# The first stage's pointwise product in three one-pass products of high and low parts, the image's low part made by VectorE

## The reference

```
xp = star_scale * square(relu(xn @ w_pw1.T)) + star_bias     # 128 -> 256 channels, the pointwise product
xf = rfft2(xp)                                               # goes on to a filter, an inverse, w_pw2
r  = relu(conv1x1(relu(conv1x1(xn, rw_fc1)), rw_conv))       # routing branch, its mean is used
s  = relu(conv3x3(xn, sp_fc1))                               # routing branch, its mean is used
```

## Time and profile before

| | before |
|---|---|
| runs | 391.28, 391.15, 389.53 us; median 391.15 |
| profiled execution, its own time | 390.03 us |
| its span on the core | 388.0 us |
| mean granted TensorE clock | 0.945 |
| TensorE busy | 84% of the span |
| VectorE / ScalarE / GpSimd busy | 59% / 44% / 57% |

### The profile page before, as it was taken

The page is one execution under the profiler, slowest core; times in us unless marked ns, Lnnn a source line. Parts: engine busy times, 40 slices in busy tenths (PEclk is TensorE's granted clock), DMA queues, the critical chain, the costliest instruction groups (busy, mean ns, idle before and its releaser), DMA issues.

```text
span 388.0 us, 7237 instructions
## 1 busy us (share of the span) xinstructions
PE 327.7 (84%) x2135; PEld 273.7 (71%) x2135; DVE 228.3 (59%) x700; ACT 170.7 (44%) x346; POOL 219.9 (57%) x257
## 2 busy tenths in 40 slices
PE   1899999995289999889685599979999999999930
PEld 0566665622158888768574599979999999999920
DVE  2376555346264479897967148785555455546844
ACT  1355544422212443328342244435645444546833
POOL 3375344030386863888877770077777777644550
PEclk9999999999589999989989699989999999999985
DMA  7990000003622324705221421123433222228535
GB/s 213 308 237 15 3 0 0 0 3 88 134 54 57 83 60 175 254 29 190 58 76 56 112 77 42 29 76 87 122 90 90 83 84 82 77 62 273 184 107 189
DMA packets 26073, 38.37 MB, mean 99 GB/s; under 512 B 5508, under 2 KB 16280, under 8 KB 25512
## 3 DMA queue, kind: packets, MB, share of 16 engines
q1 hardware_dynamic: 20408, 28.64, 26.2%
q0 software_dynamic: 4320, 8.92, 6.9%
q10 hardware_dynamic: 1312, 0.40, 0.7%
HBM read 22.16 MB, written 12.60 MB: 90 GB/s over the span
## 4 chain that ended last, share of the span: by engine, by line
PE 70%; DVE 9%; POOL 7%; DMA 6%; issue 4%; SPq 1%; ACT 1%; ACTq 0%; POOLq 0%; DVEq 0%
PE psum L1110 18%; PE psum L1094 11%; PE psum L899 8%; POOL xs_dram L641 6%; PE psum L1087 5%; PE psum L992 4%; PE psum L880 4%; PE psum L888 3%; PE psum L965 3%; PE psum L1004 2%; DMA rwc<-in_rwc 2%; PE psum L1079 2%; PE psum L911 1%; PE psum L936 1%; PE psum L986 1%
## 5 line engine op out<-in xcount | busy, mean ns | idle before, releaser
L670 POOL DMA_INDIRECT y_dram<-spec,idx_scatter x71 | 69.4, 978 | 35.1 <-issue 17.4
L641 POOL DMA_INDIRECT xs_dram<-images,idx_dispatch x64 | 62.5, 976 | 36.9 <-DVE idx_dispatch L1382 18.5
L1110 PE MATMUL psum<-RS,xgt_hl 128*128 x142 | 52.7, 371 | 6.6 <-DVE shared L1500 5.6
L817 ACT ACTIVATE shared<-psum 128x384 f32<-128x384 f32 x71 | 34.4, 489 | 46.1 <-PE psum L1110 45.9
L1500 DVE TENSOR_TENSOR shared<-shared,psum 128x384 f32<-128x384 f32 x71 | 38.3, 552 | 26.0 <-ACT shared L817 25.8
L1110 PE MATMUL psum<-w_hi,xgt_hl 128*128 x142 | 49.4, 348 | 0.0
L1506 DVE COPY spec<-psum 128x256 f32<-128x256 f32 (+1 forms) x36 | 15.1, 420 | 41.4 <-PE psum L1079 28.3
L1110 PE MATMUL psum<-w_lo,xgt_hl 128*128 x142 | 38.2, 351 | 0.0
L568 POOL TENSOR_TENSOR buf<-star 128x512 f32<-128x512 f32 (+1 forms) x8 | 10.1, 1267 | 44.9 <-DVE star L1174 44.9
L1110 PEld LDWEIGHTS psum<-RS,xgt_hl 128*128 128x128 f32 x142 | 28.1, 198 | 8.1 <-issue 8.1
L965 PE MATMUL psum<-RS,coef 128*128 128x512 f32 x48 | 20.9, 511 | 14.6 <-DMA RS<-r_dram 11.4
(11 more groups left out here) (195 smaller groups left out, 647.8 us busy)
## 6 DMA issues: line engine op xcount, KB each, us to landing
shared<-xs_dram SPq DMA_DIRECT2D x71, 65.0 KB, 1.8
star<-in_w SPq DMA_DIRECT2D x2, 1536.0 KB, 8.9
rw<-spec SPq DMA_DIRECT2D x8, 256.0 KB, 3.8
turned_b<-spec SPq DMA_DIRECT2D x8, 256.0 KB, 4.2
images<-y_dram SPq DMA_DIRECT2D x8, 256.0 KB, 4.3
out<-T SPq DMA_DIRECT2D x8, 256.0 KB, 2.0
spec<-in_w SPq DMA_DIRECT2D x1, 1536.0 KB, 6.5
shared<-in_sp_even SPq DMA_DIRECT2D x1, 1280.0 KB, 14.2
```

Of the source, the lines that this page charges most:

```text
L641: pool.indirect_dma_start(xs_dram, bass.IndirectOffsetOnAxis(ap=idx_dispatch[:, b, k, t:t + 1], axis=0), XR[:, 2 * b + t // 4, t % 4, :], ...
L670: pool.indirect_dma_start(y_dram, bass.IndirectOffsetOnAxis(ap=idx_scatter[:, j:j + 1], axis=0), yo[:, b * P:b * P + P], None).then_inc(S[ ...
L817: act.activation(silu[j % 2], p_h1[j % 2][:, 0:HID], ACT.Silu).then_inc(S["f_silu"], 1)
L1110: mm = pe.matmul(h[:, 0:HID], xgt[j // 2 % 2][xs][:, j % 2 * P:j % 2 * P + P], w_hl[ws][:, cols], start=(n == 0), stop=(n == 2))
```

## The change

`wp1` is split once into `wp1_hi` (ScalarE, a copy that rounds to `fp32r`) and `wp1_lo` (VectorE, the difference). Each pair's image is split the same way: ScalarE's first copy (L698) now writes `xc_hi` as `fp32r`, and a new VectorE operation `image_low` subtracts it from the interior of the padded image `xp` and writes the low part into `r_hl`, whose own use comes later. `image_low(i+1)` stands on VectorE between `stats(i+2)` and `spectrum_copy(i)`. `star_matmul` waits for the low part (`a_xl`) where it waited for `a_xc`, and has three products where it had one. The first routing product reads `xp`'s interior where it read `xc`. `wp1`'s transfer gets a semaphore of its own (`wp_in`); ScalarE waits for it before `image(0, 0)`, VectorE does `wp1_lo` and `image_low(0, 0)` between stats and normalise of pair 1, and TensorE waits for `wp_lo` once.

```diff
+        wp1_lo = sb("wp1_lo", [P, MED], F32R)          # in wp1's place
+        xp_s = sb("xp_s", [P, 4 * PAD * PAD + PAIRS * PIX])
+        xc_hi = sb("xc_hi", [P, 1024], F32R)
+        wp1_hl = [sb("wp1_hi", [P, MED], F32R), wp1_lo]
+        xc_hl = [xc_hi[:, :].rearrange("p (u n) -> p u n", u=2), r_hl[:].rearrange("p u f m -> p u (f m)")]
...
-        CONSTS = 16 * 8
+        CONSTS = 16 * 7
+        TERMS = ((0, 0), (0, 1), (1, 0))
...
             def image(i, u):
-                act.activation(xc[:, u, :], ps_tr[:, :], ACT.Copy).then_inc(S["a_xc"], 1)
+                act.activation(xc_hl[0][:, u, :], ps_tr[:, :], ACT.Copy).then_inc(S["a_xc"], 1)
...
             act.wait_ge(S["pad_zero"], 1)
+            act.wait_ge(S["wp_in"], 16)
+            act.activation(wp1_hl[0][:, :], wp1[:, :], ACT.Copy).then_inc(S["wp_hi"], 1)
             image(0, 0)
...
             def star_matmul(i, u):
-                pe.wait_ge(S["a_xc"], i + 1)
+                pe.wait_ge(S["a_xl"], i + 1)
                 for j in range(2):
                     wait_done(pe, S["a_relu"], i * 2 + j - 1)
                     for g in range(2):
-                        mm = pe.matmul(ps_pw[j][:, g * MED:(g + 1) * MED],
-                                       xc[:, u, (2 * g + j) * P:(2 * g + j + 1) * P], wp1[:, :], start=True, stop=True)
+                        for n, (xs, ws) in enumerate(TERMS):
+                            mm = pe.matmul(ps_pw[j][:, g * MED:(g + 1) * MED],
+                                           xc_hl[xs][:, u, (2 * g + j) * P:(2 * g + j + 1) * P], wp1_hl[ws][:, :],
+                                           start=(n == 0), stop=(n == 2))
                     mm.then_inc(S["a_pw"], 1)
...
-                                   xc[:, u, g * PIX:(g + 1) * PIX], start=True, stop=True)
+                                   xp[:, u, g, 1:SIZE + 1, 1:SIZE + 1], start=True, stop=True)
...
             pe.wait_ge(S["consts_in"], CONSTS)
+            pe.wait_ge(S["wp_lo"], 1)
             pair_loop(pe, phase_a)
...
+            def image_low(i, u):
+                dve.wait_ge(S["a_xp"], i + 1)
+                dve.wait_ge(S["a_xc"], i + 1)
+                wait_done(dve, S["a_rw1"], i - 1)
+                rows_of = "p (g a b) -> p g a b"
+                dve.tensor_tensor(xc_hl[1][:, u, :].rearrange(rows_of, g=2, a=SIZE), xp[:, u, :, 1:SIZE + 1, 1:SIZE + 1],
+                                  xc_hl[0][:, u, :].rearrange(rows_of, g=2, a=SIZE).bitcast(F32), ALU.subtract)\
+                    .then_inc(S["a_xl"], 1)
...
                     stats("a", i + 2, u)
+                if not last(i, PAIRS):
+                    image_low(i + 1, 1 - u)
+                if not deferred(i):
                     spectrum_copy(i)
...
             stats("a", 1, 1)
+            dve.wait_ge(S["wp_hi"], 1)
+            dve.tensor_tensor(wp1_hl[1][:, :], wp1[:, :], wp1_hl[0][:, :].bitcast(F32), ALU.subtract).then_inc(S["wp_lo"], 1)
+            image_low(0, 0)
             normalise("a", 1, 1)
```

More of the change, by code:

```diff
@@ L198, in metaformer @@
         route_b = sb("route_b", [P, NF * P])
-        wp1 = sb("wp1", [P, MED])
+        with nc.sbuf_tensor("wp1", [P, MED], F32) as wp1:
+            pass
+        wp1_lo = sb("wp1_lo", [P, MED], F32R)
         wp2 = sb("wp2", [P, 2, DIM])
@@ L228, in metaformer @@
         xn = sb("xn", [P, 2, 4, DIM])
-        images = sb("images", [P, 4 * PAD * PAD + PAIRS * PIX + 1024])
+        with nc.sbuf_tensor("images", [P, 4 * PAD * PAD + PAIRS * PIX + 1024], F32) as images:
+            pass
+        xp_s = sb("xp_s", [P, 4 * PAD * PAD + PAIRS * PIX])
+        xc_hi = sb("xc_hi", [P, 1024], F32R)
+        wp1_hl = [sb("wp1_hi", [P, MED], F32R), wp1_lo]
         s_from, xc_from = 4 * PAD * PAD, 4 * PAD * PAD + PAIRS * PIX
-        xp = images[:, 0:s_from].rearrange("p (u g a b) -> p u g a b", u=2, g=2, a=PAD)
-        s_all = images[:, s_from:xc_from].rearrange("p (i a b) -> p i a b", i=PAIRS, a=SIZE)
-        xc = images[:, xc_from:].rearrange("p (u n) -> p u n", u=2)
+        xp = xp_s[:, 0:s_from].rearrange("p (u g a b) -> p u g a b", u=2, g=2, a=PAD)
+        s_all = xp_s[:, s_from:xc_from].rearrange("p (i a b) -> p i a b", i=PAIRS, a=SIZE)
         XR = images[:, 0:TILES * ROW].rearrange("p (i q r) -> p i q r", q=4, r=ROW)
@@ L350, in metaformer @@
             "ident_in consts_in tab_in x_in0 x_in1 x_in2 x_in3 route_in w1_in w3_in w2_in w_hi w_lo pad_zero coef_zero mhalf_set coef_ps "
-            "coef_hi coef_lo coef_in a_stats a_aggr a_eps a_rstd a_norm a_tr a_xc a_xp a_pw a_conv a_rw1 a_relu_s "
+            "coef_hi coef_lo coef_in a_stats a_aggr a_eps a_rstd a_norm a_tr a_xl wp_in wp_hi wp_lo a_xc a_xp a_pw a_conv a_rw1 a_relu_s "
             "a_relu_r a_rw2 a_rsum a_rows a_relu a_sq a_star a_fold a_dft a_spec r_cols r_full r_taps r_mm "
@@ L427, in _ @@
                 for dst, name in consts[c]:
-                    sp.dma_start(dst[:], io[name]).then_inc(S["consts_in"], 16)
+                    sp.dma_start(dst[:], io[name]).then_inc(S["wp_in" if name == "wp1" else "consts_in"], 16)
                 i0, i1 = X_CHUNKS[c], X_CHUNKS[c + 1]
```

## The result

The changed kernel takes 387.56 us (median of 7 executions, 384.04 to 388.89) against 391.28 us for the kernel before on the same chip; the ratio is 0.9891 [0.9852, 0.9929]. It is faster by 1.1%, where 390.4 us and no measurable change were forecast. Over all executions of the two unedited kernels in this study the means are 387.6 ± 0.6 us (21) and 390.3 ± 0.2 us (145): 2.7 us, or 0.7%.

What follows compares the result with a forecast made beforehand. TensorE was taken to bound phase A. Start +0.62, pairs 1 and 2 -0.76, pairs 3 to 5 -0.24, pair 6 -0.38: together -0.76 us, 389.3 from the profiled execution, 390.4 us from the median; range 388.5 to 392.4.

Steps and rivals of the forecast that it cites:

- What phase A gains or loses is passed on whole, as everything behind it starts from its end: End of phase A: each microsecond gained or lost there was to change the kernel's time by the same amount.
- The wait inside the steps: Stars of pairs 3 to 5 waiting for `image_low`: 0.30 us stall each, bounds 0.15 and 0.55; pairs 1, 2, 6 none.
- The start: First star, waiting for `wp1_lo` and `image_low(0, 0)`: 1.0 us later, less 0.38 us saved by the star, +0.62 us.
- The product: Star in phase A: 12 `fp32r` products at 0.112 us each, 1.34 us where it took 1.73, gaining 0.38 us.
- The slower rivals: Star products: 0.17 us each, kernel 395.3 us, 10%; or weight loads not overlapped with streams, 399.6 us, 2%.
- The sum: Phase A's changes at the start and in pairs 1 to 6 added up: -0.76 us for the kernel.
- The base: Whole kernel: start from the runs' median 391.15 us, 1.1 us above the profiled execution's 390.03, giving 390.4 us.
- The copies: ScalarE's first copy of each image: same shape, only its output type changes, so no cost.
- `wp1_hi` on ScalarE: At the start: 0.4 us on ScalarE while it waits for the transposes, hidden.
- the padded reads: First routing product and `image_low` reading `xp` with gaps: no added cost.
- the queue behind `image_low`: VectorE's spectrum copies and `normalise(i+2)` in the steps: delayed, `normalise` by 0.5 us, all hidden.
- The faster rival: Stalls vanish, 0.9 us, and the clock returns sooner after TensorE's restart before phase B, 0.9 us: 388.6 us, 18%.

Runs made afterwards that it cites:

- The experiments with taps: Last step's convolution in phase A: kernel before without 3 or 6 of 9 taps, 389.3 and 389.4 us; changed kernel doing 3 taps twice, 391.0 us.

## Why the prediction was wrong

- *"What phase A gains or loses is passed on whole, as everything behind it starts from its end"*: this step failed. The experiments with taps gave 0.4, 0.7 and 2.6 us per us, the first and the last clear of one, and the change itself gave 2.7 us where phase A's net gain is 1.5. In between stand TensorE's slow stretches behind phase A, which differ from execution to execution (0.43 us less at the restart), and in three traces two dispatches on GpSimd that lasted 5 us longer together, beside VectorE's subtractions. How much of the 1.2 us each gives is only shown for the restart.
- *The wait inside the steps*, 0.30 us a pair with bounds 0.15 and 0.55: measured 0.10, below the lower bound. `image_low` started 0.07 us after the start of the last aggregate, where I had it 0.08 us after its end (0.16 us later), and took 0.66 us, and GpSimd's `var_eps` was the one held (0.50 us where it takes 0.23); so it was at the start, where the power took 1.33 us instead of 1.04 and `image_low` its 0.69. Three times 0.20 is 0.6 us. The place was right: no stall in steps 0 and 1 nor for pair 6. The changed kernel at 40 us, VectorE and GpSimd:

```profile
40.39 0.66 DVE L1200 TENSOR_TENSOR r_hl<-xp_s,xc_hi 128x512 fp32r<-128x512 f32 x1
40.63 0.50 POOL L567 TENSOR_SCALAR var_eps<-mv 128x4 f32<-128x4 f32 x1 [1.57 <-DVE mv L1173]
```

- *The start*, +0.62 us: net +0.08. The star came at 11.69 us in the profiled execution, as said, but 0.55 later on average, not 1.0, since the chunk of `x` lands at another time in each execution (at 9.32 us here, at 8.64 in the trace whose star starts at 11.04); and the star saves 0.47, not 0.38. The clock's return at "3.4 us after" was one draw from 2.9 to 5.9.
- *The product*, 0.112 us: 0.118, a star 0.31 instead of 0.38 us shorter. Right in kind, 0.07 us a star too good. The slower rivals are out: below the 0.121 us where the first begins, and no load uncovered.
- *The sum* of phase A, -0.76 us, is -1.5 (-2.05 + 0.55). That is 0.7 us of the miss of 2.8 (390.4 against 387.6); the base below is 0.8, and what came on top of phase A's gain 1.2.
- *The base*: I added 1.1 us because three executions had a median of 391.15. The mean over 145 is 390.3, so the profiled execution (390.03) was near the typical one and the forecast stood 0.8 us too high.
- *The copies, `wp1_hi` on ScalarE, the padded reads, the queue behind `image_low`*: right, nothing of them is on the chain. The faster rival, 388.6 us, was the nearest and named the restart's clock, but at 0.9 us for a restart 0.8 us earlier, where it gave 0.43, and its stalls shrank to 0.10 us instead of vanishing.

## What to carry to other kernels

Count a stage in full-clock work, its time less half of what it spent at 1.2 GHz: that repeated to 0.05 us here, where the same stage's end wandered by 2.1 us between executions of one kernel, and a single pair of traces showed no gain at all. Don't pass a stage's gain on one to one through a place where TensorE restarts or another engine has a queue; try it by lengthening and shortening the stage alone, with enough executions that the answer's interval is smaller than the gain. And take the base from many executions or from the profiled one, not from the median of three.

## What was unexpected in the hardware

- `fp32r` products of 256 columns with a full load each follow at 0.118 us: a float32 product in two records costs 0.43 us, three of these 0.35.
- The first return of the full clock fell anywhere from 13.96 to 17.57 us in the six traces of the changed kernel, and the profile's rows read 1.00 before it too.
- The changed kernel has its stretch at 1.2 GHz near 171 us, or near 260 us, in some executions and not in others.
- A GpSimd dispatch of 0.96 us took 3.4 to 3.5 us beside runs of six VectorE subtractions in three traces; in two traces of the changed kernel whose fifteenth dispatch began as long after the first subtraction (1.0 us) the two took 1.11 and 1.50 us. What makes the difference wasn't found.
